# First loads of a stage issued in the stage ahead of it, and the state-space stage's jobs in another order

## What is computed

```python
x = x + mamba(layernorm(x))       # d_inner 512, 16 states: h = dA*h + dBu over the 512 tokens
x = x + ffn(layernorm(x))         # 8 experts, top 2, capacity 80 tokens of an expert in a row
x = x + attention(layernorm(x))   # one head, causal
x = x + ffn(layernorm(x))         # the same experts again
```

## Time and profile before

| | |
|---|---|
| median of 3 runs | 3157.81 us (3155.26 to 3159.54) |
| the profiled execution's own time | 3157.39 us |
| its span in the trace | 3155.6 us |
| busy in the span: PE, DVE, POOL, ACT | 91%, 74%, 69%, 56% |
| mean granted TensorE clock | 0.954 |
| end of the state-space stage, first experts, attention | 1697, 2201, 2653 us |

### The profile page before, as it was taken

The page is one execution under the profiler, slowest core; times in us unless marked ns, Lnnn a source line. Parts: engine busy times, 40 slices in busy tenths (PEclk is TensorE's granted clock), DMA queues, the critical chain, the costliest instruction groups (busy, mean ns, idle before and its releaser), DMA issues. The chain is left out here.

```text
span 3155.6 us, 54327 instructions
## 1 busy us (share of the span) xinstructions
PE 2858.2 (91%) x16976; PEld 2264.3 (72%) x16992; DVE 2343.5 (74%) x4219; ACT 1762.2 (56%) x3333; POOL 2186.9 (69%) x1405
## 2 busy tenths in 40 slices
PE   6899989999899898999965999997999995999998
PEld 3566656666566665666655999997777774999998
DVE  3898889889898898888983666665566664666675
ACT  4776767667676677666743545543333333455453
POOL 3889988988889888899875656653244434566564
PEclk8999999999999999999987999999999997999999
DMA  5131221112211221112225554542222222545452
GB/s 160 67 116 56 83 76 63 51 61 83 73 51 50 77 83 70 42 56 76 76 111 169 120 118 123 121 109 54 68 94 91 95 92 94 121 120 121 111 125 40
DMA packets 192660, 281.60 MB, mean 89 GB/s; under 512 B 35943, under 2 KB 164622, under 8 KB 184264
## 3 DMA queue, kind: packets, MB, share of 16 engines
q1 hardware_dynamic: 157128, 236.31, 22.9%
q0 software_dynamic: 35328, 42.76, 7.6%
HBM read 197.28 MB, written 94.72 MB: 93 GB/s over the span
## 5 line engine op out<-in xcount | busy, mean ns | idle before, releaser
L627 POOL TENSOR_TENSOR dbu<-du,bb 128x1024 f32<-128x1024 f32 x512 | 1197.4, 2361 | 66.1 <-DVE hs L780 62.9
L780 DVE TENSOR_TENSOR_SCAN hs<-da,dbu 128x1024 f32<-128x1024 f32 x512 | 1145.5, 2275 | 48.8 <-POOL dbu L627 20.6
L715 ACT ACTIVATE da<-delta 128x512 f32<-128x512 f32 x1024 | 571.5, 595 | 272.5 <-DVE hs L780 252.0
L885 PEld LDWEIGHTS yT<-ident,hs 128*128 128x128 f32 x4096 | 495.2, 148 | 164.0 <-issue 113.9
L885 PE MATMUL yT<-ident,hs 128*128 128x128 f32 x4096 | 546.5, 286 | 29.0 <-DVE hs L780 28.8
L1399 POOL TENSOR_TENSOR ffn_w_lo<-ffn_w,ffn_w_hi 128x512 fp32r<-128x512 f32 x240 | 325.1, 1380 | 100.5 <-ACT ffn_w_hi L1394 100.4
L1479 PE MATMUL ffn_ybank<-ffn_w_hi,ffn_hT_hi 128*128 128x256 f32 x1280 | 364.4, 285 | 0.7 <-DVE ffn_hT_lo L1467 0.7
L1481 PE MATMUL ffn_ybank<-ffn_w_hi,ffn_hT_lo 128*128 128x256 f32 x1280 | 359.4, 281 | 0.0
L1480 PE MATMUL ffn_ybank<-ffn_w_lo,ffn_hT_hi 128*128 128x256 f32 x1280 | 359.1, 281 | 0.0
L1445 PE MATMUL ffn_hbank<-ffn_rowsT_hi,ffn_w_hi 128*128 128x320 f32 x1024 | 339.0, 331 | 3.8 <-DVE ffn_rowsT_lo L1433 2.3
L1456 ACT ACTIVATE ffn_hT_hi<-ffn_hbank,ffn_b 128x320 fp32r<-128x320 f32 x512 | 268.9, 526 | 113.1 <-PE ffn_hbank L1447 113.1
(11 more groups left out here) (242 smaller groups left out, 5226.4 us busy)
## 6 DMA issues: line engine op xcount, KB each, us to landing
bb<-b_rows SPq DMA_DIRECT2D x64, 1024.0 KB, 4.6
ffn_w<-L_ffn_W SPq DMA_DIRECT2D x60, 1024.0 KB, 6.5
slots<-empty SPq DMA_DIRECT2D x40, 530.0 KB, 6.9
ffn_rows<-slots SPq DMA_DIRECT2D x32, 662.5 KB, 4.9
a_x<-x_after_mamba SPq DMA_DIRECT2D x32, 512.0 KB, 5.8
xt<-L_attn_a_x SPq DMA_DIRECT2D x16, 512.0 KB, 4.1
x<-L_attn_a_x SPq DMA_DIRECT2D x16, 512.0 KB, 4.0
x_after_mamba<-x SPq DMA_DIRECT2D x16, 512.0 KB, 2.9
```

The lines of the kernel that those rows point to most:

```text
L627: pool.tensor_tensor(dbu[:, s % DEEP], du[:, dt, :].unsqueeze(1).to_broadcast([P, SN, T]), bb[:, q * SN:(q + 1) * SN, :], ALU.mult).then_i ...
L715: ins = act.activation(da[:, s % 2, i, :], delta[:, par, dt, :], ACT.Exp, scale=-float(q * SN + i + 1))
L780: dve.tensor_tensor_scan(flat[0], flat[1], flat[2], 0.0, ALU.mult, ALU.add).then_inc(scanned.sem, 1)
L885: mm = pe.matmul(yT[:, j * P:(j + 1) * P], hs[:, s % DEEP, i, j * P:(j + 1) * P], k.ident[:], start=False, stop=(q == QS - 1 and i == SN - ...
```

## The change

- The first expert's rows and bias are loaded at the end of the stage ahead (`load_first_rows`), into buffers that live through all stages (`k.first_rows` is the tile that held the zeros for clearing; it grew from 4 to 5 rows of slots). SP waits until the first 8 rows' sends have landed; expert 0's first turn reads only these. In the expert stage SP waits for `rows_ld` and passes it on (`first_loads`).
- The last row's eight sends leave the stage ahead. POOL issues them in the expert stage's first turn, behind `take_parts` and ahead of the low weights for turn 1 (`send_last`). Before the loads for the second half of the batch SP waits until all sends have landed. For this POOL's first two turns stand outside its loop.
- Attention's rows 0 and 1 are loaded in the first expert stage, ahead of the attention weights, after a wait for the additions of turn 7. They land in the tile of the old `w_x`, which also takes the first expert's second weight; so in attention SP waits for the last row's norm ahead of `load_first`.
- In the state-space stage the jobs stand behind other steps on ACT, DVE, PE and POOL, and in another order in the ring. No job is added or removed.

The diff, cut to its core; in the parts `if s == ...` the indentation is cut too, in the order POOL, ACT, DVE, PE. What is left out only renames a tile's index.

```diff
-        self.xn, self.xnT = sb("r_xn", [P, copies, NT, ROW]), sb("r_xnT", [P, NC, T])
+        self.xn = [sb("r_xn", [P, NT, ROW])] * (copies - 1) + [k.last_xn]
+        self.xnT = sb("r_xnT", [P, NC, T])
...
-        self.send = sb("r_send", [P, NT * K], U32)
+        self.send = k.last_send
...
-        self.sent = Count(sem("r_sent"), 16 * NT * K)
+        self.sent = Count(k.sent[nth - 1], 16 * NT * K)
...
-RING_JOBS = ("G3", "Z0", "U2", "T0", "O0", "T1", "U3", "I0", "O1", "I1", "G0", "Z1", "I2", "I3", "S", "RT0", "RT1",
-             "DA0", "DA1", "DA2", "DA3", "G1", "RL", "U0", "Z2", "U1", "G2", "Z3", "RP", "-")
-MM_JOBS = ("G3", "Z0", "U2", "T0", "O0", "T1", "U3", "I0", "I1", "O1", "G0", "Z1", "I2", "I3", "S", "RT0", "RT1",
-           "DA0", "DA1", "DA2", "DA3", "G1", "RL", "U0", "Z2", "U1", "G2", "Z3", "RP")
-ACT_JOBS = ("U2", "T0", "T1", "U3", "S", "RT0", "RT1", "DA0", "DA1", "DA2", "DA3", "U0", "U1")
-DVE_JOBS = ("G3", "Z0", "O0", "I0", "O1", "G0", "I1", "Z1", "I2", "I3", "G1", "RL", "Z2", "G2", "RP", "Z3")
+RING_JOBS = ("G3", "Z0", "U2", "O0", "T0", "T1", "U3", "I0", "I1", "O1", "G0", "Z1", "I2", "I3", "S", "RT0", "RT1",
+             "DA0", "DA1", "DA2", "DA3", "G1", "RL", "U0", "Z2", "U1", "G2", "RP", "Z3", "-")
+MM_JOBS = ("G3", "Z0", "U2", "O0", "T0", "T1", "U3", "I0", "I1", "O1", "G0", "Z1", "I2", "I3", "RT0", "RT1", "S",
+           "DA0", "DA1", "DA2", "DA3", "G1", "RL", "U0", "Z2", "U1", "G2", "RP", "Z3")
+ACT_JOBS = ("U2", "T0", "T1", "U3", "RT0", "S", "RT1", "DA0", "DA1", "DA2", "DA3", "U0", "U1")
+DVE_JOBS = ("G3", "Z0", "O0", "I0", "I1", "O1", "G0", "Z1", "I2", "I3", "G1", "RL", "Z2", "G2", "RP", "Z3")
...
+    k.att_x = flat_b[:, 0:2 * NT * C].rearrange("p (a j c) -> p a j c", a=2, c=C)
+    k.att_x_ld = sem("att_x_ld")
+    k.empty, k.first_b2 = sb("empty", [P, NR, ROW]), sb("first_b2", [P, C])
+    k.first_rows = k.empty
+    k.last_xn, k.last_send = sb("last_xn", [P, NT, ROW]), sb("last_send", [P, NT * K], U32)
+    k.rows_ld, k.sent = sem("rows_ld"), [sem("sent1"), sem("sent2")]
-    k.empty = sb("empty", [P, 4, ROW])
...
+def load_first_rows(sp, k, w, nth):
+    sp.wait_ge(k.sent[nth - 1], 16 * NT * K * HALF)
+    slots = (k.slots1, k.slots2)[nth - 1]
+    sp.dma_start(k.first_rows[:], slots[0:ROWS].rearrange("(r p) c -> p r c", p=P)).then_inc(k.rows_ld, 16)
+    sp.dma_start(k.first_b2[:], w["b2"][0].partition_broadcast(P)).then_inc(k.rows_ld, 16)
+def send_last(pool, k, nth):
+    for n in range(NT * K):
+        pool.indirect_dma_start(
+            (k.slots1, k.slots2)[nth - 1], bass.IndirectOffsetOnAxis(ap=k.last_send[:, n:n + 1], axis=0),
+            k.last_xn[:, n // K, :], None, bounds_check=SLOTS - 1, oob_is_err=False).then_inc(k.sent[nth - 1], 16)
...
+                load_first_rows(sp, k, w, 1)
...
-if s == 17 and has_first(turn + 1):
+if s == 16 and has_late(turn):
+    prompt_rstd(pool, r.norm, turn - 2)
+if s == 22 and has_first(turn + 1):
     prompt_rstd(pool, norm, turn + 1)
-if s == 17 and has_late(turn):
-    prompt_rstd(pool, r.norm, turn - 2)
-if s == 28 and has_first(turn):
+if s == 30 and has_first(turn):
     softplus(pool, turn, par, 1)
-if s == 29 and has_first(turn):
     softplus(pool, turn, par, 2)
-if s == 30 and has_first(turn):
+if s == 31 and has_first(turn):
     softplus(pool, turn, par, 3)
...
-                for n in range(NT * K):
-                    route_send(pool, r, B - 1, n)
-                pool.wait_ge(r.sent.sem, r.sent.at(B - 1, 16 * NT * K))
+                pool.wait_ge(r.sent.sem, r.sent.at(B - 2, 16 * NT * K))
...
-if s == 0 and late:
+if s == 1 and late:
     gate_input(act, turn, 3)
-if s == 1 and late:
     summed_copy(act, turn, turn - 2, 3)
-if s == 4 and main:
+if s == 5 and main:
     skip_input(act, turn, row, 2)
-if s == 5 and first:
+if s == 6 and first:
     for c in range(NC):
         turned(act, turn, par, c)
-if s == 7 and first:
+if s == 7 and main:
+    skip_input(act, turn, row, 3)
+if s == 8 and first:
     conv_input(act, turn, 0)
-if s == 8 and main:
-    skip_input(act, turn, row, 3)
-if s == 10 and main:
+if s == 9 and main:
     summed_copy(act, turn, row, 0)
-if s == 11 and first:
-    tanh_x(act, turn, 0)
+if s == 9 and first:
     conv_input(act, turn, 1)
 if s == 12 and first:
+    tanh_x(act, turn, 0)
+if s == 13 and first:
     tanh_x(act, turn, 1)
...
-if s == 16 and late:
-    route_apply(act, turn, turn - 2)
-if s == 18 and main:
-    summed_copy(act, turn, row, 1)
+if s == 17 and late:
+    route_apply(act, turn, turn - 2)
+    route_turned(act, turn, 0)
+if s == 19 and main:
+    summed_copy(act, turn, row, 1)
 if s == 19 and late:
-    route_turned(act, turn, 0)
-if s == 20 and first:
+if s == 21 and first:
     step_size(act, turn, par, 0)
-if s == 21 and first:
     step_size(act, turn, par, 1)
     step_size(act, turn, par, 2)
+    step_size(act, turn, par, 3)
+if s == 23 and first:
     exp_part(act, turn, 0)
-if s == 23 and first:
-    step_size(act, turn, par, 3)
+    exp_part(act, turn, 1)
 if s == 24 and first:
-    exp_part(act, turn, 1)
-if s == 26 and main:
-    gate_input(act, turn, 2)
+if s == 24 and late:
+    route_exp(act, r, turn - 2)
-if s == 28 and has_first(turn + 1):
+if s == 28 and main:
+    gate_input(act, turn, 2)
+if s == 30 and has_first(turn + 1):
     prompt_apply(act, norm, xt, xt, turn + 1)
-if s == 29 and late:
-    route_exp(act, r, turn - 2)
...
     silu_z(dve, turn, 3)
-    gate(dve, turn, 3)
-if s == 2 and main:
+if s == 2 and late:
+    gate(dve, turn, 3)
+if s == 3 and main:
     silu_z(dve, turn, 0)
-if s == 3 and main:
     step_input(dve, turn, row, 1 - par, 2)
-if s == 3 and late:
+if s == 4 and late:
     residual(dve, turn, turn - 2, 0)
-if s == 6 and main:
+if s == 5 and main:
     step_input(dve, turn, row, 1 - par, 3)
-if s == 9 and first:
-    silu_x(dve, turn, 0)
-if s == 10 and late:
-    residual(dve, turn, turn - 2, 1)
-if s == 12 and main:
-    gate(dve, turn, 0)
-if s == 12 and first:
-    silu_x(dve, turn, 1)
-if s == 12 and is_turn(turn, 0):
+if s == 10 and is_turn(turn, 0):
     dve.wait_ge(loaded, 16 * CONSTS)
     dve.tensor_tensor(b_skip[:], b_u[:], d_skip[:], ALU.mult).then_inc(skip_ready, 1)
     dve.wait_ge(k.shaped, KIT_SHAPED)
+if s == 11 and first:
+    silu_x(dve, turn, 0)
+if s == 12 and first:
+    silu_x(dve, turn, 1)
+if s == 12 and late:
+    residual(dve, turn, turn - 2, 1)
 if s == 13 and main:
-    silu_z(dve, turn, 1)
+    gate(dve, turn, 0)
-if s == 15 and first:
+if s == 15 and main:
+    silu_z(dve, turn, 1)
+if s == 16 and first:
     silu_x(dve, turn, 2)
-if s == 16 and first:
     silu_x(dve, turn, 3)
-if s == 22 and main:
+if s == 23 and main:
     gate(dve, turn, 1)
-if s == 26 and main:
+if s == 28 and main:
     silu_z(dve, turn, 2)
-if s == 30 and first:
+if s == 31 and first:
     step_input(dve, turn, turn, par, 1)
...
-if s == 1 and first:
-    turn_x(pe, turn, 0)
 if s == 2 and first:
+    turn_x(pe, turn, 0)
+if s == 3 and first:
     turn_x(pe, turn, 1)
-if s == 5 and late:
-    out_proj(pe, turn, 2)
-if s == 7 and first:
+if s == 7 and late:
+    out_proj(pe, turn, 2)
+if s == 8 and first:
     conv_taps(pe, turn, 0)
-if s == 7 and late:
+    conv_taps(pe, turn, 1)
+if s == 8 and late:
     out_proj(pe, turn, 3)
-if s == 8 and first:
-    conv_taps(pe, turn, 1)
+if s == 10 and main:
     in_proj(pe, turn, 1 - par, "Z1", ND + 1)
+if s == 10 and first:
+    in_proj(pe, turn, par, "I2", 2)
 if s == 11 and first:
-    in_proj(pe, turn, par, "I2", 2)
+if s == 11 and is_turn(turn, 0):
+    pe.wait_ge(loaded, 16 * CONSTS)
-if s == 13 and is_turn(turn, 0):
-    pe.wait_ge(loaded, 16 * CONSTS)
-if s == 14 and first:
     x_proj_small(pe, turn, 0)
+if s == 13 and late:
+    route_turn(pe, turn, turn - 2, 0)
+if s == 14 and late:
+    route_turn(pe, turn, turn - 2, 1)
-if s == 15 and late:
-    route_turn(pe, turn, turn - 2, 0)
-    route_turn(pe, turn, turn - 2, 1)
+if s == 17 and first:
+    dt_proj(pe, turn, 2)
 if s == 18 and first:
-    dt_proj(pe, turn, 2)
-if s == 18 and is_turn(turn, 2):
+if s == 19 and is_turn(turn, 2):
     pe.wait_ge(route_loaded, 16 * ROUTE_CONSTS)
     pe.wait_ge(k.shaped, KIT_SHAPED)
-if s == 19 and main:
+if s == 20 and main:
     turn_back(pe, turn, row, 1)
-if s == 19 and late:
+if s == 20 and late:
     route_score(pe, turn)
-if s == 20 and first:
+if s == 22 and first:
     x_proj(pe, turn, 0, 0)
-if s == 22 and first:
     x_proj(pe, turn, 0, 1)
-if s == 22 and main:
+if s == 23 and main:
     in_proj(pe, turn, 1 - par, "Z2", ND + 2)
     turn_back(pe, turn, row, 2)
-    in_proj(pe, turn, 1 - par, "Z3", ND + 3)
+if s == 30 and main:
+    in_proj(pe, turn, 1 - par, "Z3", ND + 3)
                 turns(pe, one_turn)
...
-        def load_first_rows(sp):
-            for dst, src in ((rows[:, 0], slots[0:ROWS].rearrange("(r p) c -> p r c", p=P)),
-                             (b2[:, 0], w["b2"][0].partition_broadcast(P))):
-                sp.dma_start(dst, src).then_inc(loaded[0].sem, 16)
```

(36 more changed lines are left out.)

42 lines of the change are left out of this document (21 added, 21 removed).

## The result

The changed kernel takes 3117.83 us (median of 4 runs, 3116.45 to 3119.79) where the kernel before, run beside it, takes 3156.53 (3148.87 to 3159.54): a ratio of 0.9881, 95% interval 0.9863 to 0.990, or 38.7 us less. The forecast was 3103, with 3074 to 3131 as its range. The profiled execution has a span of 3118.0, against 3155.6 before: 37.6 us less, and that difference is what is taken apart here.

The account below looks back on a forecast made before the run. PE bounds the expert stages except where it stands still; the state-space stage is a chain between engines. 13.8 + 3.9 + 17.1 + 20 = 54.8 off 3157.4 gives 3102.6, forecast 3103 us, range 3074 to 3131.

Parts of the forecast that it names:

- the rival of the neutral order: State-space stage: the new job order gains nothing, giving 3123 us; chance 0.20.
- First hand-over: State-space stage to first expert stage: PE's first product comes sooner, saving 13.8 us, bounds 11 to 16.
- SP now also waits for the clearing transfers: First hand-over: clearing runs to about 1681.4, so SP issues the rows at 1681.5 and the first product starts at 1691.7.
- Second, 3.9: First expert stage to attention: only the landing of attention's row goes, saving 3.9 us, between 3.4 and 4.2.
- Third, 17.1: Attention to second expert stage: barrier opens when DVE is done, POOL's low weights come next; saves 17.1 us, 15 to 18.
- The sends cost 0: Expert stages, turn 0: eight moved sends take 10.2 us on POOL, covered with 11 us left before turn 1.
- the rival of turn 1 held up: Expert stages: sends over 2.6 us each beside DVE's splitting delay turn 1 by 6 us per stage: 3115; chance 0.04.
- The order, 20 us: State-space stage: reordered jobs save 1.3 us in each of 15 turns plus 0.5 for the first fill.
- The bound from POOL's row of sends: State-space turn: POOL's ninth product ends 29.7 us after the first scan, so scan 9 can't start earlier in either order.
- the sign of being wrong: State-space stage, new profile: the two neighbouring scan turns staying at 99.5 and 101.6 us would refute the forecast.
- The fill: State-space stage, first turn: the new order was to save 0.5 us there.
- The rival with PE stopped ahead of RT0: State-space stage: PE waits for ScalarE's late norm, making the kernel slower, 3170 us or 3202; chance 0.05.

Follow-up runs that it names:

- the kernel with all edits: The changed kernel with first weights loaded later, clears a turn earlier, sends in the third expert turn, two normalised-row tiles and padded slots: ratio 0.9858, 3110.8 us.
- spacer: The kernel before with one unused SBUF tile, in two runs: 6356 bytes, ratio 0.9992; 32 bytes, ratio 0.999, 3154.3 us.

## Why the prediction was right or wrong

The direction and the range held, and of the three hand-overs the second and third; the forecast of 3103 was 15 us too low, and the time is nearest to the rival of the neutral order (3123). That the range held is in part luck: the hand-overs gave 4 us more than the sum had, and the order gave 17 less and the expert stages lost 6, which no term held. With the late ScalarE the time is 3129, 2 us inside the bound.

- *First hand-over, 13.8 (11 to 16):* 17.6. The step that failed is "SP now also waits for the clearing transfers", and only together with the new order: with the old one the first product stands 10.25 behind the slots, as said, and the saving is 13.8. The prediction took the slots' and the clearing's times from the kernel before, though its own order moves both. From the last scan the clearing starts 2.2 us earlier, since the store of the last row does, and the slots come 6.9 later. So the rows were there in time and the low weights decided, as in the third hand-over; the 3.8 us gained here lie within the 7 lost ahead of the slots: from the last scan to the first product it is 44.9 us with the old order and 48.1 with the new.
- *Second, 3.9:* 3.6. *Third, 17.1:* 17.7, with the first product 6.5 behind the slots where 7.0 was said. The split is shown too: 4 us for the loads, 13.5 for the sends.
- *The sends cost 0:* their own cost was right. They take 0.977 us (median of 16) with gaps of 0.30, and turn 1 doesn't wait for them. The rule weighed against it did not show: the figure of the Trainium skill (SBUF — State Buffer, section "SBUF: two separate sides"), 3100 ns for a transfer beside a two-port DVE operation, appears at none of them. What is measured is POOL's instruction, since the trace has no landing of these sends, and no run here was made to put a two-port operation beside them. But the place is not free everywhere: on two chips ScalarE was late beside the sends, for 11 us in all. No term of the sum held that; its size is near the rival of turn 1 held up (12 us), by another mechanism than the one named.
- *The order, 20 us:* this is the mis-sized term. It measured 2 us by itself (5 less to 1 more), and about 3 by the stretches. The bound from POOL's row of sends was read one step off: the product at 861.95 is that of step 3 (counted from 0), and in that turn POOL's product for step 9 ends 26.2 us behind the first scan, not 29.7. Scan 9 still starts at 29.6 there in both kernels, held by other waits. In the neighbouring turns, of 101 us, the bound holds: scan 9 starts 29.2 and 29.3 us into the turn, 0.1 behind POOL's product. The upper bound is a slip too: 3 us in 15 turns are 45, not 47. The wait for `tanh_x` is gone as said, but "1.3 us of each of 15 turns" was 0.3: a late decay and a late `x_proj` took its place, where a wait for POOL's product had been expected, and the wait for the logarithm stayed at 2.78 (2.91 before). The turns of 101.2 and 98.9 lie nearer to the 101.6 and 99.5 named as the sign of being wrong than to the 100.5 and 98 forecast. The fill gave 5.5 and not 0.5.
- *What the order cost, which the sum lacked:* 7 us behind the last scan; 3.9 came back with the weights' load moved, and all of it where ScalarE's wait for the landing was taken out as well (32.7 us in the kernel with all edits, 34.65 before). The prediction moved `Z3` on DVE and PE, and left out that SP waits for `Z3` before it loads the first weights. The rival with PE stopped ahead of RT0 didn't come: that gap is under 0.5 us in all turns but the last two, where it is 10.7 and 16.3 us.
- *Expert turns:* 30.08 before and 30.25 after (mean of 28 turns, the first and last of each stage left out), 5.2 us in 30 turns. The second product's matmuls have 287, 281 and 282 ns against 285, 280 and 281. It is in all nine kernels run here that have the loads and rows of the change, wherever the sends stand, and in neither spacer. What is left are edits that no run took apart, the rows and biases as tiles of their own and POOL's turns written out among them; the cause stays open.

## What to carry to other kernels

Work that a stage's last step leaves behind (sends, the next stage's first loads) is worth moving over the barrier: the saving is the whole distance to the next late thing. It could be read from the timelines of the kernel before to within a microsecond, as long as nothing else of the change moved those times; where the new order moved them, the reading was 3.8 us off. An order that removes an engine's waits gains only what the next producer isn't late by: here three engines are busy nine tenths of a turn, 6.5 us of waits a turn were removed, and 0.3 us was gained. And when a job is moved, follow everybody who waits for it, the queue that issues loads too: a load that starts 4 us later can lie over a pause of another engine and lengthen it.

## What the runs showed of the hardware

- Between two indirect sends behind the last scan POOL stood 3.4 to 3.6 us in six executions, and 4.9 and 5.3 us in two, with hardly any other transfer beside it; it stood 8.1 to 8.4 us in the six executions in which 2 MB of weight loads lay over the pause. In each pause one packet of 16 KB went over an instruction queue. That POOL waited for it is a reading.
- The last of those eight sends landed 3.7 us behind its start in the kernel before, with the queue of SP's transfers at 71% of the DMA engines' time beside it, and 5.7 and 6.7 us behind it with that queue at 92% and 93% (clears a turn earlier, and the changed kernel; by the start of ScalarE's norm, which waited for it).
- Beside eight scattered sends and a load at 0.95 of the DMA engines' time, ScalarE took up finished tiles up to 2.4 us late on two chips, and on time in the first run of the same program; the ratio moved from 0.9881 to 0.9911. What holds ScalarE isn't in the trace. Two gaps of 1.8 and 1.7 us on PE, with one tile between them, were followed by 6.8 us at half its clock.
